# Second and third layer of the edge network: four 64x64 quadrant products against full-array products by a block-diagonal weight

## The chip, the cores and the metric

One core of a Trainium2 chip runs the whole program. Its engines are TensorE (PE in the views, with PEld for the loads of its stationary operand), VectorE (DVE), ScalarE (ACT), GpSimd (POOL) and the queues that start DMAs (SP and POOL). The metric is the device time of one execution in microseconds. The time before is the median of three runs.

## The reference, cut to what matters

Four stages follow one another on 1250 nodes of 512 features and 40000 edges: a segment mean, a mixture of experts, a graph network on the edges, and a second mixture of experts. The change lies in the third, in the small network that turns the 8 features of every edge into 512 weights:

```python
h = edge_feats                                   # [40000, 8]
for W in (W_mlp1, W_mlp2, W_mlp3):               # 8x64, 64x64, 64x64
    h = SILU_2MOM * jax.nn.silu(h @ W / jnp.sqrt(jnp.float32(W.shape[0])))
tpw = h @ W_mlp4 / jnp.sqrt(jnp.float32(W_mlp4.shape[0]))   # [40000, 512]
w1, w2, w3, w4 = jnp.split(tpw, 4, axis=-1)
s0 = x0[sender]; s1 = x1[sender]
# p1..p4: products of w1..w4 with the sender's features and the edge's 4 attributes
msg0 = jax.ops.segment_sum(m0, receiver, num_segments=num_nodes)
msg1 = jax.ops.segment_sum(m1, receiver, num_segments=num_nodes)
```

Everything is float32. The second and third layer multiply 64 hidden features by a 64x64 weight.

## The kernel before, in words

The edges are sorted by receiver into 352 tiles of 128 edges (`NTILE`). Four tiles make a step (`Q`, 88 steps, `STEPS`), eight a batch of the network (`BT`, 44 batches, `NB`). The loop over the steps is one pipeline of five engines.

**Network, layers 0 to 3 (`mlp_product`, L1686 on TensorE; `mlp_function`, L1326 on ScalarE).** Layer 0 turns the features of two batches round with one transpose (L1690). Layer 1 is four products with 64 rows of the array (L1696). The result of a batch is `act1`, 128 partitions by 512: partitions 0 to 63 hold the 64 hidden features of one half of the batch's 1024 edges, partitions 64 to 127 those of the other half. Layers 2 and 3 (both L1703) use four quadrants of 64x64 of the array: for each half `k` of the columns and each row half `h` a product of 64 rows, 64 columns of output and 256 moving columns, written to partitions 64k of bank 6 or 7 (the two banks of `pairs[3]`). So each of the two layers exchanges the places of edges between partitions and columns, and after both they are back. After each layer ScalarE applies silu from PSUM to `act1` (L1332), `act2` (L1334) or `act3` (L1336), one instruction of 128 by 512. A float32 product shows in the trace as two instructions on PE, each with its own load on PEld; the four quadrants of a layer show as 8 instructions.

**Last layer (`weights_of`, L1741).** For two tiles at a time it makes the 512 weights per edge in two banks: 64 rows, 128 columns of output, 512 moving columns, twice. A step has two such calls. Call `i` waits until VectorE is through with the messages of four tiles before (`v_msg`), as those four banks are a ring of two pairs.

**Messages (VectorE, `messages_of`, L1045 and L1048).** For two tiles at a time the weights in PSUM are multiplied by the gathered rows of the senders. It waits for `weights_of` (`p_tp`) and for the two gathers (`d_gat`). Once a step `picks_of` (L1032) and once in four steps `hot_of` (L1021) make parts of the stationary operand of the sum.

**Sum (TensorE, `sum_up`, L1758 and L1761).** For every step the messages are summed to 32 nodes by products with 32 columns of output, in four column tiles of the array. ScalarE then copies the sums out and scales what is carried on (L1403, L1406), and makes its share of the picks (L1391).

**Gathers (GpSimd, L1953).** One indirect DMA per tile into a ring of 8 tiles (`NGAT`); gather `i` waits until the messages of tile `i - 8` are made.

The order on TensorE in step `s` (L1765 and after) is: `weights_of` twice, then the products of the network that `mlp_order` (L146) gives to the gap of this step, then `sum_up(s - 1)`. With r = s // 2 + 1, an even step's gap holds layer 1 of batch r + 1 and layer 3 of batch r; an odd step's gap holds layer 2 of batch r + 1 and, in every second odd step, layer 0 of batches r + 2 and r + 3. Before the loop five places (L1724) hold the layers of batches 0 and 1 with which the loop begins, each after ScalarE's part of the place before. `spin` (L1473) issues products of 128x128 by 512 float32 columns whose results nobody reads: seven in step 0, three in step 88.

Of the kernel before, what the change touches and what calls it, by code (L numbers as in the profile page):

```python
# [13 lines left out]
ACT = mybir.ActivationFunctionType  # L14
# [37 lines left out]
MUL, HID = 128, 64  # L52
SILU_2MOM = 1.679177
# [4 lines left out]
ARENA = 42960  # L58
ZONE = HB * (4096 + 2048)
NW3 = 3  # L60
LATE = 2 * MUL + 2 * HID + 512 + 512
assert NB % 2 == 0 and NB * 64 + 2 * NTILE <= 4 * NPAD - LATE
NGAT, NSUM, NPICK, NHOT, HOT_STEPS = 8, 3, 3, 2, 4
PICKED = 2
# [93 lines left out]
def program(nc, consts, x, anc, sub, leaf_table, src, dst, ea4, ea8, gate, w13, w2, w_up, w_mlp1, w_mlp23,  # L158
            w_mlp4, w_out, ew, ei, v1, v2, out):
    ctx = ExitStack()  # L160
    with ctx:

        def sem(name):
            return ctx.enter_context(nc.semaphore(name))
# [7 lines left out]
        def carve(words, at=None):  # L172

            if at is None:
                at, top[0] = top[0], top[0] + words
                assert top[0] <= ARENA, top[0]
            return arena[:, at:at + words]

        def zone_of(at, size):

            used = [0]

            def take(words):
                used[0] += words
                assert used[0] <= size, (used[0], size)
                return carve(words, at + used[0] - words)

            return take

        def phase_tensors(**sizes):  # L190

            with ExitStack() as phase:
                return [phase.enter_context(nc.sbuf_tensor(n, [128, words], dt))[:, :]
                        for n, (words, dt) in sizes.items()]

        pairs = [ctx.enter_context(nc.psum_tensor(f"pair{i}", [128, 1024], F32)) for i in range(4)]
        banks = [pair[:, h * 512:(h + 1) * 512] for pair in pairs for h in range(2)]
# [103 lines left out]
        _, other_down1 = phase_tensors(other_gap1=(2048, F32), other_down1=(2048, F32))  # L301
        spare = zone_of(lnT_at, 4 * NPAD - LATE)
        other_spare, xS, hS = spare(2048), spare(512), [spare(512) for _ in range(2)]
# [3 lines left out]
        acc = dram("node_sums", [N + TILE, D])  # L307
        e_w = [carve(2048, zone + ZONE - 2048), carve(2048, edge_at)]
        late = zone_of(lnT_at + 4 * NPAD - LATE, LATE)
        wup_sb, m23_sb, m4_sb, wo_sb = late(2 * MUL), late(2 * HID), late(512), late(512)  # L310

        recs = carve(NREC * REC, edge_at).rearrange("p (s c) -> p s c", c=REC)
        table = dram("node_table", [N, 4 * MUL])
# [16 lines left out]
        act1, act2, fT, act3 = ring(512), ring(512), ring(128), [ring(512) for _ in range(2)]  # L330
# [4 lines left out]
        sum_pair, tp_pair, mlp_pair = pairs[0], pairs[1:3], pairs[3]  # L335
        tp_bank = banks[2:6]
        mlp_halves = mlp_pair[:, :].rearrange("p (h x) -> p h x", h=2)
        mlp_out = (banks[7][:, 256:384], mlp_halves[:, :, 0:256], mlp_halves[:, :, 0:256], mlp_halves[:, :, 256:512])
        oz = zone_of(zone, ZONE)
        sums_T = [oz(8 * MUL) for _ in range(2)]  # L340

# [57 lines left out]
        a_pick, a_mlp = sem("last_picks_made"), sem("mlp_activated")  # L399
# [759 lines left out]
        def scalar(a):  # L1159
# [63 lines left out]
            for k in range(NG):  # L1223
                if k >= 4:
                    a.wait_ge(p_start, k - 3)
                for c in range(4):
                    done = a.activation(out=diag[k % 4][:, c], in_=ident[:EP, :EP], func=ACT.Identity,
                                        scale=start_part[:, c % 2 * NW + 2 * k + c // 2:c % 2 * NW + 2 * k + c // 2 + 1])
# [97 lines left out]
            def mlp_function(r, layer):  # L1326
                b = mlp_out[layer]
                a.wait_ge(p_prod, mlp_done[r, layer])
                if layer == 0:
                    a.activation(out=fT, in_=b, func=ACT.Copy).then_inc(a_mlp, 1)  # L1330
                elif layer == 1:
                    a.activation(out=act1.rearrange("p (h x) -> p h x", h=2), in_=b, func=ACT.Silu, scale=8 ** -0.5).then_inc(a_mlp, 1)  # L1332
                elif layer == 2:
                    a.activation(out=act2.rearrange("p (h x) -> p h x", h=2), in_=b, func=ACT.Silu, scale=SILU_2MOM / 8).then_inc(a_mlp, 1)  # L1334
                else:
                    a.activation(out=act3[r % 2].rearrange("p (h x) -> p h x", h=2), in_=b, func=ACT.Silu,  # L1336
                                 scale=SILU_2MOM / 8).then_inc(a_mlp, 1)
# [42 lines left out]
            for place in mlp_first:  # L1380
                for r, layer in place:
                    mlp_function(r, layer)
# [27 lines left out]
            for s in range(STEPS + 1):  # L1410
                for r, layer in mlp_gaps[s] if s < STEPS else []:
                    mlp_function(r, layer)
                if s:
                    carry(s - 1)
                if s + 1 < STEPS:
                    picks_of(s + 1)
# [9 lines left out]
            def split_out(e):  # L1426
                if e:
# [6 lines left out]
                         scale=3 ** -0.5).then_inc(a_p4, 1)  # L1434
            for u in range(NT + 1):
# [5 lines left out]
                for h in range(2):  # L1441
                    done = a.activation(out=sums_T[u % 2][:, h * 512:(h + 1) * 512], in_=banks[2 * (u % 2) + h][:, :],
                                        func=ACT.Copy)
                done.then_inc(a_sums_T, 1)
                if u - 2 in TURNS_AT:
# [3 lines left out]
                                 in_=banks[6 + t % 2][:, :].rearrange("p (k n) -> p k n", k=4),  # L1449
                                 func=ACT.Copy).then_inc(a_xt, 1)  # L1450
# [18 lines left out]
        def tensor(pe):  # L1469
# [6 lines left out]
            for t in range(NT):  # L1476
                mm = pe.matmul(out=banks[2][:, t:t + 1], lhsT=in_sub[:, t * NP:(t + 1) * NP].bitcast(F32), rhs=K["sub512"],
                               start=True, stop=True)
# [9 lines left out]
            for t in range(NT):  # L1488
                if t >= 3:
                    pe.wait_ge(v_hit, t - 2)  # L1490
                if t == 7:
# [4 lines left out]
                          start=True, stop=True).then_inc(p_key, 1)  # L1496
# [14 lines left out]
            for t in range(NT):  # L1511
                g = slice(t % Q * WN, t % Q * WN + WN)
                pe.wait_ge(a_ln, t + 1)
                mm = pe.matmul(out=banks[0][g, :], lhsT=in_bound[:, t * WN:(t + 1) * WN], rhs=ln[:, t], start=t < Q,
                               stop=t + Q >= NT, skip_group_check=True)
            mm.then_inc(p_parts, 1)
            for t in range(NT):
                if t >= 3:
# [5 lines left out]
                          stop=True).then_inc(p_seg, 1)  # L1524
# [14 lines left out]
            for t in range(NT):  # L1539
# [3 lines left out]
                for k in range(4):  # L1543
                    mm = pe.matmul(out=banks[2][:, t * E0:(t + 1) * E0], lhsT=lnT[:, k, t * NP:(t + 1) * NP],
                                   rhs=gate_sb[:, k], start=k == 0, stop=k == 3)
# [3 lines left out]
                      skip_group_check=True)  # L1549
            pe.matmul(out=banks[6][:, E0:NT * E0], lhsT=ones, rhs=so_far_t[:, 0:NT - 1], start=False, stop=True,  # L1550
                      skip_group_check=True)
            pe.matmul(out=banks[7][:, 0:E0], lhsT=ones, rhs=so_far_t[:, NT - 1], start=True,
                      stop=True).then_inc(p_before, 1)
# [4 lines left out]
                      stop=True).then_inc(p_before, 1)  # L1558
            for k in range(NG):
                pe.wait_ge(a_diag, k + 1)  # L1560
                for c in range(4):
                    mm = pe.matmul(out=banks[3 + c // 2][:EP, 0:EJ], lhsT=diag[k % 4][:, c], rhs=marks[:, k],
                                   start=k + c % 2 == 0, stop=k == NG - 1 and c % 2 == 1)
# [123 lines left out]
            def mlp_product(r, layer):  # L1687
                b = mlp_out[layer]
                if layer == 0:
                    mm = pe.transpose(out=b, in_=feat[:, r * 64:(r + 2) * 64], identity=ident)  # L1690
                elif layer == 1:
                    for k in range(2):
                        q = r % 2 * 2 + k
                        for h in range(2):
                            p = slice(64 * h, 64 * (h + 1))
                            mm = pe.matmul(out=b[:, h, k * 128:(k + 1) * 128], lhsT=m1_sb[p, q * 128:(q + 1) * 128],  # L1696
                                           rhs=fT[p], start=True, stop=True, skip_group_check=True)
                else:
                    w, given = (m23_sb[:, 0:HID], act1) if layer == 2 else (m23_sb[:, HID:2 * HID], act2)
                    for k in range(2):  # L1700
                        for h in range(2):
                            p = slice(64 * h, 64 * (h + 1))
                            mm = pe.matmul(out=b[64 * k:64 * (k + 1), h], lhsT=w[p],  # L1703
                                           rhs=given[p, k * 256:(k + 1) * 256], start=True, stop=True,
                                           skip_group_check=True)
                return mm

            pe.wait_ge(a_y, FT)
# [3 lines left out]
            for t in range(NT):  # L1712
# [6 lines left out]
                for k in range(4):  # L1719
                    mm = pe.matmul(out=banks[2 + s][:, k * 128:(k + 1) * 128], lhsT=nT[s][:, k * 128:(k + 1) * 128],  # L1720
                                   rhs=wup_sb[:, 0:MUL] if k == 0 else wup_sb[:, MUL:2 * MUL], start=True, stop=True)
                mm.then_inc(p_up, 1)
            pe.wait_ge(g_packed, 4)
            for place in mlp_first:  # L1724
                if mlp_ahead[place[0]]:
                    pe.wait_ge(a_mlp, mlp_ahead[place[0]])
                for r, layer in place:
                    mm = mlp_product(r, layer)
                mm.then_inc(p_prod, 1)
# [39 lines left out]
            for s in range(STEPS + 1):  # L1769
                if s < STEPS:  # L1770
                    for i in range(s * Q, (s + 1) * Q, 2):
                        weights_of(i)
                    if mlp_gaps[s]:
                        pe.wait_ge(a_mlp, mlp_ahead[mlp_gaps[s][0]])
                        for r, layer in mlp_gaps[s]:
                            mm = mlp_product(r, layer)
# [50 lines left out]
            for t in range(NT):  # L1827
# [10 lines left out]
                for extra in extra_hl:  # L1838
                    mm = pe.matmul(out=bank[:, :], lhsT=extra_hot[t], rhs=extra, start=False, stop=True,
                                   skip_group_check=True)  # L1840
# [7 lines left out]
            for e in range(E1):  # L1848
                pe.wait_ge(v_w1, e + 1)
                for h in range(2):  # L1850
                    if e:
                        pe.wait_ge(a_gelu, 2 * (e - 1) + h + 1)
                    for k in range(4):
                        for a, b in PASSES:
                            mm = pe.matmul(out=banks[2 + h][:, :], lhsT=a1_hl[:, a, k, h * 128:(h + 1) * 128],  # L1855
                                           rhs=x_hl[:, b, k], start=k + a + b == 0, stop=k == 3 and a == 1)
                    mm.then_inc(p_h, 1)
                pe.wait_ge(v_w2, e + 1)
                for k in range(2):
                    pe.wait_ge(v_h, 2 * e + k + 1)  # L1860
                    for t in range(T5):
                        n = e * T5 + t
                        if e and k == 0:
                            pe.wait_ge(v_y, n - T5 + 1)
                        for a, b in PASSES:
                            mm = pe.matmul(out=banks[4 + n % 4][:, :], lhsT=h_hl[k][:, a, t * NP:(t + 1) * NP],  # L1866
                                           rhs=a2_hl[:, b, k], start=k + a + b == 0, stop=k == 1 and a == 1)
# [348 lines left out]
```

## Time and profile before

| | us |
|---|---|
| median of three runs (lowest, highest) | 1435.27 (1434.62, 1439.81) |
| the profiled execution, its own time | 1440.99 |
| its span, first to last instruction | 1439.1 |
| PE, PEld busy | 1353.6, 833.0 |
| DVE, ACT, POOL busy | 1151.2, 1003.0, 922.4 |

The page gives busy time per engine and the span in 40 slices. Matmuls are pipelined and their ends are modelled, so the busy time of PE contains the overlap with the next group; the distance from one group's start to the next group's start says what a group really takes. The loop over the steps runs from 833.2 us to 1305 us of the span.

### The profile page before, as it was taken

What the parts mean: (1) busy time and instruction counts of PE and PEld (TensorE: products, weight loads), DVE (VectorE), ACT (ScalarE), POOL (GpSimd) and SP (SyncE); (2) the same over time, 40 slices, a digit from 0 to 9 for tenths busy, and PEclk for the clock granted to TensorE, in tenths of its full rate; (3) what the DMA queues carried; (4) which work ended last, traced back from release to release, by engine and by line L of the source; (5) the groups of instructions that cost most, each with busy time, mean ns of one, the idle gap of its engine ahead of it and who ended that gap; (6) DMA issues with size and microseconds to landing.
All of it is one profiled execution on the core that took longest, in us unless ns stands there. A gap on an engine that the chain in (4) does not pass through costs nothing.

```text
span 1439.1 us, 24478 instructions
## 1 busy us (share of the span) xinstructions
PE 1353.6 (94%) x8774; PEld 833.0 (58%) x8774; DVE 1151.2 (80%) x1459; ACT 1003.0 (70%) x2000; POOL 922.4 (64%) x762
## 2 busy tenths in 40 slices
PE   4957999999899999999999699999999999998999
PEld 3454746888378874888567534434444443336887
DVE  7888927999089972999459769999999999995665
ACT  6237726888178863888457459999999999884433
POOL 4226675888888888888883467777777777762000
PEclk9859999999999999999999999999999999999999
DMA  9429476277827566765622769989999999985421
GB/s 331 155 92 334 134 243 239 37 272 278 294 34 282 187 232 187 281 215 158 182 62 49 238 189 306 306 296 307 309 305 303 307 307 293 294 291 176 144 89 59
DMA packets 91601, 316.54 MB, mean 220 GB/s; under 512 B 23754, under 2 KB 25988, under 8 KB 80859
## 3 DMA queue, kind: packets, MB, share of 16 engines
q1 hardware_dynamic: 45832, 202.57, 37.7%
q0 software_dynamic: 45648, 112.41, 28.7%
q8 instruction: 70, 1.15, 0.3%
q14 instruction: 51, 0.42, 0.1%
HBM read 378.96 MB, written 77.16 MB: 317 GB/s over the span
## 4 chain that ended last, share of the span: by engine, by line
PE 70%; DVE 11%; DMA 8%; POOL 5%; issue 4%; ACT 1%; SPq 0%; DVEq 0%; POOLq 0%; ACTq 0%
PE pair L1599 32%; PE pair L1741 7%; PE pair L1636 4%; PE pair L1761 4%; DMA arena<-node_table,arena 4%; POOL arena L1953 4%; DVE arena L1048 3%; PE pair L1758 3%; PE pair L1855 3%; PE pair L1866 3%; PE pair L1653 3%; PE pair L1703 2%; PE pair L1590 2%; POOL pair_rows L1906 1%; DVE arena L1045 1%
## 5 line engine op out<-in xcount | busy, mean ns | idle before, releaser
L1916 POOL DMA_INDIRECT sorted_edges<-arena x311 | 460.1, 1480 | 104.2 <-issue 96.0
L910 DVE TENSOR_TENSOR weights_hl<-arena,weights_hl 128x1024 fp32r<-128x1024 f32 x342 | 405.3, 1223 | 62.3 <-ACT weights_hl L1242 59.7
L1953 POOL DMA_INDIRECT arena<-node_table,arena x352 | 340.7, 968 | 129.6 <-issue 89.4
L1242 ACT ACTIVATE weights_hl<-arena 128x1024 fp32r<-128x1024 f32 x342 | 351.9, 1060 | 46.6 <-PE pair L1599 46.4
L1599 PE MATMUL pair<-weights_hl,rows_hl 128*128 128x512 f32 x1368 | 325.9, 395 | 4.3 <-ACT weights_hl L1242 3.0
L1048 DVE TENSOR_TENSOR arena<-pair,arena 128x1536 f32<-128x1536 f32 x176 | 307.7, 1748 | 0.0
L1599 PEld LDWEIGHTS pair<-weights_hl,rows_hl 128*128 128x128 f32 x1368 | 251.7, 188 | 69.8 <-DVE weights_hl L910 10.5
L1741 PE MATMUL pair<-arena 64*128 64x512 f32 x704 | 185.3, 634 | 7.2 <-DVE arena L1048 7.0
L1599 PE MATMUL pair<-weights_hl,hidden_hl 128*128 128x512 f32 x684 | 165.7, 395 | 0.0
L1391 ACT ACTIVATE arena<-arena 128x32 f32<-128x32 bf16 x704 | 157.8, 314 | 0.0
L1045 DVE TENSOR_TENSOR arena<-pair,arena 128x512 f32<-128x512 f32 x176 | 120.8, 686 | 29.5 <-PE pair L1741 19.8
L1599 PEld LDWEIGHTS pair<-weights_hl,hidden_hl 128*128 128x128 f32 x684 | 125.0, 188 | 25.6
L1761 PE MATMUL pair<-arena 128*32 128x256 f32 x2112 | 130.1, 379 | 0.0
L929 DVE TENSOR_TENSOR arena<-pair,arena 128x512 f32<-128x512 f32 x69 | 47.3, 686 | 101.8 <-ACT arena L1280 74.0
L1403 ACT ACTIVATE arena<-pair 128x512 f32<-128x512 f32 x176 | 105.1, 597 | 30.2 <-PE pair L1758 22.0
L1761 PEld LDWEIGHTS pair<-arena 128*32 128x32 f32 x2112 | 68.6, 110 | 82.9 <-issue 52.7
L1406 ACT ACTIVATE pair<-pair,arena 128x512 f32<-128x512 f32 x174 | 114.8, 660 | 0.0
L1741 PEld LDWEIGHTS pair<-arena 64*128 64x128 f32 x704 | 55.4, 186 | 99.8 <-DVE arena L1048 58.6
L1280 ACT ACTIVATE arena<-pair 128x512 f32<-128x512 f32 x69 | 41.3, 599 | 101.6 <-PE pair L1636 87.9
L1758 PE MATMUL pair<-arena 128*32 128x512 f32 x704 | 93.7, 604 | 0.0
L1636 PE MATMUL pair<-arena 128*64 128x512 f32 x352 | 88.9, 614 | 2.8 <-DMA arena<-in_w 2.8
L1926 POOL DMA_INDIRECT node_sums<-arena x27 | 52.2, 1932 | 51.4 <-ACT arena L1288 36.5
(292 smaller groups left out, 1541.0 us busy)
## 6 DMA issues: line engine op xcount, KB each, us to landing
arena<-in_w SPq DMA_DIRECT2D x73, 2048.0 KB, 8.6
arena<-in_w SPq DMA_DIRECT2D x85, 1024.0 KB, 9.2
sums<-arena SPq DMA_DIRECT2D x88, 512.0 KB, 5.7
other_down<-in_w SPq DMA_DIRECT2D x8, 1024.0 KB, 12.2
arena<-in_v SPq DMA_DIRECT2D x16, 512.0 KB, 4.6
pair_rows<-arena SPq DMA_DIRECT2D x1, 5934.0 KB, 26.2
arena<-pair_rows SPq DMA_DIRECT2D x23, 256.0 KB, 3.9
arena<-node_table,arena POOLq DMA_INDIRECT x352
```

What stands on the lines that cost most here:

```text
L910: v.tensor_tensor(out=part[s][:, 1], in0=by_chunk(n)[4], in1=part[s][:, 0].bitcast(F32), op=ALU.subtract).then_inc(v_low, 1)
L1045: v.tensor_tensor(out=m[:, :, 0:2], in0=w12, in1=rows_in[:, :, 0:1].to_broadcast([128, 2, 2, MUL]), op=ALU.mult)
L1048: v.tensor_tensor(out=m[:, :, 2:8].rearrange("p t (w m) u -> p t w (m u)", w=2), in0=w34.unsqueeze(2).to_broadcast([128, 4, 3, MUL]), in1= ...
L1242: a.activation(out=part[s][:, 0], in_=cols, func=ACT.Copy).then_inc(a_high, 1)
L1391: done = a.activation(out=picks[s % NPICK][:, j, c], in_=hot[s // HOT_STEPS % NHOT][:, s % HOT_STEPS, j], func=ACT.Copy, scale=recs[:, j * ...
L1599: mm = pe.matmul(out=bank[:, :], lhsT=st[:, a], rhs=part[s][:, w, half * 512:(half + 1) * 512], start=begins and (a, w) == (0, 0), stop=en ...
L1636: mm = pe.matmul(out=banks[2 + 2 * s + c][HALF * h:HALF * (h + 1), :], lhsT=xS[:, at:at + HALF], rhs=w[:, c], start=k == 0, stop=k == 3, s ...
L1741: mm = pe.matmul(out=tp_bank[(i + h) % Q], lhsT=act3[batch % 2][p, k * 128:(k + 1) * 128], rhs=m4_sb[p], start=True, stop=True)
L1758: mm = pe.matmul(out=bank, lhsT=pick, rhs=m[:, 1:5], start=s == 0, stop=True, skip_group_check=True)
L1761: mm = pe.matmul(out=bank.rearrange("p (b u) -> p b u", b=4)[:, c - 1:4:4 - c], lhsT=pick, rhs=m[:, 0:c + 5:c + 4], start=s == 0 and c == ...
L1916: g.indirect_dma_start(out=sorted_edges, out_offset=bass.IndirectOffsetOnAxis(ap=slot_i[:, j:j + 1], axis=0), in_=er[:, j, :], in_offset=N ...
L1953: g.indirect_dma_start(out=row, out_offset=None, in_=table, in_offset=bass.IndirectOffsetOnAxis(ap=senders[:, i:i + 1], axis=0)).then_inc( ...
```

## The change

The weights of layers 2 and 3 come from the host as two block-diagonal matrices of 128x128: W2 (or W3) at rows and columns 0 to 63 and again at 64 to 127. A batch's layer 2 becomes one product of 128 rows, 128 columns of output and 512 moving columns into bank 6, and layer 3 two products of 128x128 and 256 moving columns, into banks 6 and 7. Edges no longer change places between the two layers. The weight tile in SBUF grows from 128 to 256 columns; the tiles beside it move. ScalarE's silu of layer 2 reads one bank of 512 columns, where it read 256 columns of each of two.

```diff
-LATE = 2 * MUL + 2 * HID + 512 + 512
+LATE = 2 * MUL + 4 * HID + 512 + 512
@@
-        wup_sb, m23_sb, m4_sb, wo_sb = late(2 * MUL), late(2 * HID), late(512), late(512)
+        wup_sb, m23_sb, m4_sb, wo_sb = late(2 * MUL), late(4 * HID), late(512), late(512)
@@
-        mlp_out = (banks[7][:, 256:384], mlp_halves[:, :, 0:256], mlp_halves[:, :, 0:256], mlp_halves[:, :, 256:512])
+        mlp_out = (banks[7][:, 256:384], mlp_halves[:, :, 0:256], banks[6], mlp_halves[:, :, 256:512])
@@
-                    a.activation(out=act2.rearrange("p (h x) -> p h x", h=2), in_=b, func=ACT.Silu, scale=SILU_2MOM / 8).then_inc(a_mlp, 1)
+                    a.activation(out=act2, in_=b[:, :], func=ACT.Silu, scale=SILU_2MOM / 8).then_inc(a_mlp, 1)
@@
+                elif layer == 2:
+                    mm = pe.matmul(out=b[:, :], lhsT=m23_sb[:, 0:128], rhs=act1, start=True, stop=True)
                 else:
-                    w, given = (m23_sb[:, 0:HID], act1) if layer == 2 else (m23_sb[:, HID:2 * HID], act2)
-                    for k in range(2):
-                        for h in range(2):
-                            p = slice(64 * h, 64 * (h + 1))
-                            mm = pe.matmul(out=b[64 * k:64 * (k + 1), h], lhsT=w[p],
-                                           rhs=given[p, k * 256:(k + 1) * 256], start=True, stop=True,
-                                           skip_group_check=True)
+                    for h in range(2):
+                        mm = pe.matmul(out=b[:, h], lhsT=m23_sb[:, 128:256], rhs=act2[:, h * 256:(h + 1) * 256],
+                                       start=True, stop=True)
@@
-        w_mlp23=np.tile(np.concatenate([g["W_mlp2"], g["W_mlp3"]], 1), (2, 1)),
+        w_mlp23=np.concatenate([at_blocks((128, 128), g[f"W_mlp{n}"], [(0, 0), (HID, HID)]) for n in (2, 3)], 1),
```

## Rows read from the trace of the kernel before

**Rows 1.** Loop, busy time: stretch, length, PE, PEld, DVE, ACT, POOL, clock, DMA.
```profile
844.80:1285.70 440.90, 436.09 (x4387) 176.95 (x4388) 424.98 (x440) 403.11 (x1146) 323.45 (x334) 1.00 0.90 298
```

**Rows 2.** Chain of waits, one stretch of four steps: start us, us, what.
```profile
980.87 1.92 PE pair L1741 x8
982.78 0.59 PE pair L1703 x8
983.38 0.26 PE pair L1690
...
985.92 1.95 PE pair L1741 x8
...
988.32 0.59 PE pair L1703 x8
...
991.20 2.13 PE pair L1741 x8
...
996.22 1.99 PE pair L1741 x8
...
1001.54 0.62 PE pair L1741
```

**Rows 3.** Who waited for whom in the loop: total us, times, longest.
```profile
DVE arena L1045 <- PE pair L1741: 12.5, 19, 5.2
PE pair L1741 <- DVE arena L1048: 4.7, 7, 1.1
DVE arena L1045 <- DMA arena<-node_table,arena: 4.1, 6, 1.2
```

**Rows 4.** VectorE in order of time: start us, us, line, operation.
```profile
982.07 0.69 DVE L1045 TENSOR_TENSOR arena<-pair,arena 128x512 f32<-128x512 f32 x1 [0.42 <-PE pair L1741]
...
984.35 0.68 DVE L1045 TENSOR_TENSOR arena<-pair,arena 128x512 f32<-128x512 f32 x1
...
986.61 0.42 DVE L1032 TENSOR_TENSOR arena<-arena 128x256 f32<-128x256 bf16 x1
986.94 0.69 DVE L1021 TENSOR_TENSOR arena<-arena 128x512 bf16<-128x512 bf16 x1
987.54 0.68 DVE L1045 TENSOR_TENSOR arena<-pair,arena 128x512 f32<-128x512 f32 x1
```

**Rows 5.** TensorE in order of time: the spin of step 0, narrow windows.
```profile
838.63 6.28 PE L1473 MATMUL pair<-arena 128*128 128x512 f32 x14
...
843.89 1.02 PE L1473 MATMUL pair<-arena 128*128 128x512 f32 x2
...
844.32 0.59 PE L1473 MATMUL pair<-arena 128*128 128x512 f32 x1
844.84 1.99 PE L1741 MATMUL pair<-arena 64*128 64x512 f32 x8
```

**Rows 6.** TensorE: full-array products of 128 columns, then a transpose.
```profile
823.71 1.78 PE L1720 MATMUL pair<-arena 128*128 128x128 f32 x14
825.33 0.27 PE L1690 MATMUL pair<-arena 128*128 128x128 f32 x1
```

**Rows 7.** Instructions of TensorE in the loop by line.
```profile
L1703 PE MATMUL pair<-arena 64*64 64x256 f32 x672 | 55.7, 402 | 0.0
L1690 PE MATMUL pair<-arena 128*128 128x128 f32 x20 | 6.6, 328 | 0.0
```

**Rows 8.** VectorE, first message of step 1 and of step 85.
```profile
846.47 0.69 DVE L1045 TENSOR_TENSOR arena<-pair,arena 128x512 f32<-128x512 f32 x1 [5.18 <-PE pair L1741]
...
1285.74 0.69 DVE L1045 TENSOR_TENSOR arena<-pair,arena 128x512 f32<-128x512 f32 x1 [0.24 <-DMA arena<-node_table,arena]
```

**Rows 9.** TensorE before the loop and in step 0.
```profile
831.77 1.13 PE L1703 MATMUL pair<-arena 64*64 64x256 f32 x8 [1.21 <-ACT arena L1336]
832.83 0.47 PE L1690 MATMUL pair<-arena 128*128 128x128 f32 x1
...
837.80 0.90 PE L1703 MATMUL pair<-arena 64*64 64x256 f32 x8
```

## The prediction, made before the changed kernel ran

> **What bounds the kernel now.** I read the busy times of the loop first: it takes 440.9 us of the span from 844.8 to 1285.7, and PE is busy 436.1 of it, VectorE 425.0, ScalarE 403.1, GpSimd 323.5 [rows 1]. The reader is to see that two engines are within 4% of full, so that busy time alone can't say which of them sets the pace. GpSimd's figure leaves out the time between its gathers.
>
> Then the chain of waits over four steps in the middle [rows 2]. In steady running it stays on TensorE. The starts of the four blocks of `weights_of` (L1741) at 980.87, 985.92, 991.20, 996.22 and 1001.54 give steps of 5.05, 5.28, 5.02 and 5.32 us, together 20.67. I use these four steps as the unit, because they hold two batches of the network: two layers 2, two layers 3, two layers 1, one layer 0.
>
> How much of the 20.67 does TensorE wait? The block after 980.87 lasts 1.92 and the same block after 991.20, with the same kind of group behind it, 2.13: 0.21 of waiting there. The two blocks in front of layer 1 last 1.95 and 1.99. One such block is four streams of 0.43 and one load of 0.11 (below), 1.83; 0.10 more belongs to it in this view, since the chain begins the next group of the same shape 0.1 later than it starts; so 0.02 and 0.06 are waits. Sum 0.3 us; TensorE without any wait would need 20.67 - 0.3 = 20.37.
>
> VectorE's own need [rows 4]: a pair of messages takes 984.35 - 982.07 = 2.28 and 986.61 - 984.35 = 2.26, the picks 986.94 - 986.61 = 0.33, and once in four steps the one-hot 987.54 - 986.94 = 0.60. Four steps need 4 x (2.27 + 2.27 + 0.33) + 0.60 = 20.08. That is 0.3 us less than TensorE's need, and the first row shows which one is late: the first message of the step waited 0.42 us for `weights_of`. Over the whole loop the waits say the same [rows 3]: the messages waited 12.5 us for `weights_of` and 4.1 us for gathers, `weights_of` 4.7 us for messages. TensorE sets the pace, with little to spare behind it.
>
> The unit doesn't hold everywhere. From the first message of step 1 at 846.47 to that of step 85 at 1285.74 are 439.3 us [rows 8] for 84 steps or 21 units; 21 x 20.67 = 434.1. The other 5.2 us are stretches in which a gather lands late and VectorE then is late for TensorE.
>
> **Price of the new products.** A layer is now 8 instructions on four quadrants, 0.59 us from its start to the next group's; so both for the layer 2 at 982.78 and the layer 3 at 988.32 [rows 2], and 672 instructions or 84 groups of it lie in the loop [rows 7]. What the new form costs is told best by the spin, which has its shape: 128 rows, 128 columns of output, 512 float32 columns, two instructions each [rows 5]. From the start at 843.89 to that at 844.32 are 0.43 us per instruction. From the first start 838.63 to the last 844.32 are 5.69, which is 13 x 0.43 and 0.1: before the first stream a load of the weights is exposed, 0.11. From the last start to the next group of another shape are 844.84 - 844.32 = 0.52, 0.09 more than the stream. So a full-array product alone between groups of other shapes costs 0.11 + 2 x 0.43 + 0.09 = 1.06 us.
>
> Layer 2 in a step without layer 0: 0.59 becomes 1.06, +0.47. Layer 2 in front of layer 0: today 0.59 + 0.26 = 0.85 [rows 2]. The transpose has the shape of the new product. Where it follows such products today, 14 products of 128 columns and the transpose start evenly (825.33 - 823.71 = 1.62, 0.115 each), with no load to be seen in front of it [rows 6]; so its 0.26 falls to 0.15 and the layer's 0.09 goes: 0.97 + 0.15 = 1.12, +0.27. Layer 3: two products of 256 columns, four instructions of half the stream, 0.11 + 4 x 0.215 + 0.09 = 1.06, +0.47. No row shows a full-array product of 256 columns. From below, with no exposed load and no gap at either end, it is 0.86, +0.27; from above, if each of the two products paid its load and its gap, 0.86 + 0.4 = 1.26, +0.67. I take +0.47, as the stream goes with the columns between the rows of 128 (0.115) and 512 (0.43).
>
> The Trainium skill (TensorEngine Tiling (Array Packing), Key Properties) has that a change of tiling mode, not only of tile, drains TensorE. The 0.09 and 0.11 around the spin agree. By that rule the change takes one of the two switches around every second layer 2 away, which is the 0.2 by which that case is cheaper, and alters nothing else in number.
>
> **What the loop makes of it.** A unit of TensorE's work becomes 20.37 + 0.27 + 0.47 + 2 x 0.47 = 22.05 us. VectorE's stays 20.08, so it has 2 us per unit to spare and TensorE's 0.3 of waiting goes: the step with the one-hot needs 5.47 on VectorE, and TensorE's own step there is 5.05 + 0.27 = 5.32, 0.15 shorter, but the next one is 5.75, and two steps of PSUM lie between the two. So 22.05 against 20.67, +1.38 for a unit and +29.0 for 21. Late gathers: what waits for a gather is VectorE, mostly by about 1 us or less (longest 1.2 of 6 waits [rows 3]), and 2 us of slack in a unit take nearly all of that; of the 5.2 us I leave 0.5, -4.7. GpSimd has more time per gather, ScalarE too; its silu waits for the end of the gap's products and then runs while `sum_up` does, as now. Loop: +24.3.
>
> Before the loop the layers are on the path, each waiting for ScalarE [rows 9]. Layers 2 and 3 of batch 0 come at full speed, +0.47 each until the result. Layer 2 of batch 1 at 831.77 runs at the clock's lower level (1.2 GHz in place of 2.4): to the transpose at 832.83 are 1.06 us for the 8 instructions that take 0.59 in the loop. The new one needs 0.11 + 2 x 0.86 = 1.83, less 0.11 of load in front of the transpose, +0.65. Sum 1.6. In step 0 the layer 3 at 837.80 took 0.83 (to the spin at 838.63), partly at half clock; new 1.06 at full and 2.0 at half, +0.2 to +1.2, of which 0.4 disappear because the message at 846.47 [rows 8] came 0.4 after the product before it was done (844.84 + 0.11 + 2 x 0.43 + 0.16, what an instruction lasts beyond its stream, [rows 5]). I take +1.4 for all before step 1, with 0.8 and 2.6 as ends.
>
> After step 85 no products of the network remain, and the last three steps wait for gathers: nothing. The larger weight tile adds 64 KB to one transfer that is issued long before the loop: nothing, 0.2 us if it were waited for. ScalarE's silu from one bank in place of two: 512 columns as before, nothing.
>
> Sum: +24.3 + 1.4 = +25.7 us. The profiled execution took 1440.99 (span 1439.1), so its like is 1466.7 (span 1464.8). The median of the three runs is 5.7 lower: 1435.3 + 25.7 = **1461.0**.
>
> **Rivals.**
> *Hidden, not slower.* VectorE or the ring of gathers sets the pace, and TensorE's longer gap falls into its waiting. For it: VectorE busy 96%, DMA 0.90, late gathers. Against it: TensorE's waits are 0.3 us in 20.67 and it would have to take 1.65. It decides where TensorE's need for a unit stays under the 20.67 of now; the price then is 0 to 1.4, 1435 to 1437. The Trainium skill (Perfetto Trace Analysis, Identifying the Most-Contended Engine) calls matmul busy time a bad measure of TensorE's load and wants that of the weight loads in its place. Here the loads are busy 177.0 of 440.9 us, 40% [rows 1], by which VectorE would be the bound and this rival true. The distances of starts speak against that. Chance 4%.
>
> *Cheaper switches.* The load and the gap around the new products hide as they do between groups of one shape: 0.86 for each, +0.27 in place of +0.47 for 22 layers 2 alone and 42 layers 3, -12.8, and 0.2 less before the loop: +13, 1448. For it: the load of the next weights is hidden inside the spin. Against: the spin's own first load is not. Chance 9%.
>
> *Nothing given back.* Late gathers and waits for messages stay what they are: 22 x 0.47 + 20 x 0.27 + 42 x 0.47 = +35.5 in the loop and up to 2.6 before it, 1473. It would hold if the ring of gathers were tied to TensorE's order by more than messages. Chance 8%. Products of 256 columns at the upper price of 1.26 give 42 x 0.2 = 8.4 more, 1469; 4%.
>
> **How the numbers follow.** The forecast has 75%, its own range 1455 to 1467. The range that should hold 8 in 10 leaves out most of the first, half of the second and the worst of the last rivals: 1450 to 1469. A difference of 0.5%, 7.2 us, is what can be told from no change here (the three runs span 5.2 us). Slower by more than that: all but the hidden case, 0.95; within it 0.04; faster 0.01, since no part takes anything from any engine but 0.1 us of load before every second layer 0.
>
> **What would show it.** Right: line by line, the layer 2 group as 2 instructions and 1.06 us to the next start, layer 3 as 4 and 1.06, the transpose 0.15; a unit of four steps of 22.0 to 22.1 us; VectorE waiting for `weights_of` in every step, some 35 us over the loop in place of 12.5, and for gathers under 2; `weights_of` waiting for messages under 2. Wrong: a unit that stays near 20.7, VectorE without longer waits, or groups of 0.86.

## The result, and the profile after

| | before | after |
|---|---|---|
| median, us (lowest, highest; 4 runs each) | 1435.78 (1434.62, 1439.81) | 1460.22 (1459.27, 1463.27) |
| the profiled execution, its own time, us | 1440.99 | 1459.27 |
| its span, us | 1439.1 | 1457.3 |

The ratio is 1.0175, 95% interval 1.0156 to 1.0194: slower by 24.4 us. The forecast was 1461.0 and slower.

Chain of waits of the changed kernel, four steps, where [rows 2] has those of before. Line 1739 is `weights_of`, 1699 layer 2, 1702 layer 3, 1690 layer 0:

```profile
981.85 1.92 PE pair L1739 x8
983.76 1.05 PE pair L1699 x2
984.82 0.11 PE pair L1690
...
987.22 1.92 PE pair L1739 x8
...
989.58 1.06 PE pair L1702 x4
...
992.93 1.92 PE pair L1739 x8
994.85 1.06 PE pair L1699 x2
...
998.20 1.92 PE pair L1739 x8
...
1003.91 1.92 PE pair L1739 x8
```

Read two things here. The groups of two and four instructions last 1.05 and 1.06 us where the eight quadrant instructions lasted 0.59. And all blocks of `weights_of` last 1.92 us, where before they had 1.92, 1.95, 2.13 and 1.99: TensorE waits for nobody. From 981.85 to 1003.91 are 22.06 us, against 20.67.

The waits in the loop of the changed kernel, total us, times, longest (to compare with [rows 3]), and its busy times ([rows 1]):

```profile
POOL arena L1951 <- DVE arena L1048: 60.9, 85, 1.2
...
DVE arena L1045 <- PE pair L1739: 36.0, 62, 1.0
...
DVE arena L1045 <- DMA arena<-node_table,arena: 1.9, 3, 0.9
...
PE pair L1739 <- DVE arena L1048: 0.6, 1, 0.6
```
```profile
844.80:1303.30 458.50, 457.92 (x3920) 203.18 (x3920) 421.23 (x436) 405.48 (x1141) 321.87 (x333) 1.00 0.89 286
```

These waits are taken up to 1308 us, a little behind the loop; up to 1303.3 us, as far as [rows 3] goes in the kernel before, they are 35.6 (61 times), 1.3 (2 times) and 0.6. So VectorE's wait for `weights_of` went from 12.5 to 35.6 us, that for gathers from 4.1 to 1.3, TensorE's for messages from 4.7 to 0.6. The weight loads are busy 203 of 458 us, 44%, in a stretch in which TensorE has no gap left.

The loop's ends in VectorE's order of time, as in [rows 8]:

```profile
839.87 0.69 DVE L1045 TENSOR_TENSOR arena<-pair,arena 128x512 f32<-128x512 f32 x1 [4.83 <-PE pair L1739]
...
1303.33 0.69 DVE L1045 TENSOR_TENSOR arena<-pair,arena 128x512 f32<-128x512 f32 x1 [0.32 <-PE pair L1739]
```

463.5 us in place of 439.3: the loop took 24.2 more. 21 x 22.06 = 463.3, so the 5.2 us that the loop took beyond its undisturbed units, put down to late gathers, fell to 0.2.

The whole of the two profiled executions: up to the start of layer 0 of batches 0 and 1 (825.33 before, 817.71 after) the changed kernel is 7.6 us earlier, in stages that the change doesn't touch; from there to the first message of step 1 it takes 22.2 us in place of 21.1, +1.0; in the loop +24.2; behind it +0.6. Since layer 0 that is +25.8. The 7.6 us go the other way, and these two executions differ by only 18.3 us; the medians differ by 24.4. Runs of the kernel before spread over 5 us by themselves.

### The profile page after: what moved, and what is told of

The parts are those of the page before. It is cut to its first block, busy times and chain, and to the rows that moved or that the text cites. A ratio compares the mean times of both kernels' runs of the same rounds, so it can differ in the third digit from the quotient of the medians.

```text
span 1457.3 us, 23598 instructions
## 1 busy us (share of the span) xinstructions
PE 1379.8 (95%) x8334; PEld 862.1 (59%) x8334; DVE 1152.0 (79%) x1459; ACT 1008.6 (69%) x2000; POOL 918.4 (63%) x762
## 4 chain that ended last, share of the span: by engine, by line
PE 84%; DVE 6%; DMA 4%; POOL 2%; issue 2%; ACT 1%; SPq 0%; DVEq 0%; POOLq 0%; ACTq 0%
PE pair L1599 32%; PE pair L1739 11%; PE pair L1759 7%; PE pair L1756 6%; PE pair L1636 5%; PE pair L1702 3%; PE pair L1699 3%; PE pair L1853 3%; PE pair L1864 3%; PE pair L1653 3%; PE pair L1590 2%; POOL pair_rows L1904 1%; PE pair L1696 1%; PE pair L1805 1%; DMA arena<-node_table,arena 1%
## 5 line engine op out<-in xcount | busy, mean ns | idle before, releaser
L1739 PE MATMUL pair<-arena 64*128 64x512 f32 x704 | 176.5, 618 | 3.5 <-DVE arena L1048 3.5
L1739 PEld LDWEIGHTS pair<-arena 64*128 64x128 f32 x704 | 60.4, 186 | 83.9 <-issue 55.7
L1636 PE MATMUL pair<-arena 128*64 128x512 f32 x352 | 85.8, 599 | 0.3 <-DMA arena<-in_w 0.3
```

What stands on the lines that cost most here:

```text
L1636: mm = pe.matmul(out=banks[2 + 2 * s + c][HALF * h:HALF * (h + 1), :], lhsT=xS[:, at:at + HALF], rhs=w[:, c], start=k == 0, stop=k == 3, s ...
L1739: mm = pe.matmul(out=tp_bank[(i + h) % Q], lhsT=act3[batch % 2][p, k * 128:(k + 1) * 128], rhs=m4_sb[p], start=True, stop=True)
```

## The experiments

They ran on several chips, and the kernel before shows two times: on three chips, called slow below, it takes 1604.8, 1616.4 and 1615.8 us, on the others 1436 to 1437. Each kernel is compared with the kernel before on its own chip. "Unit" is the time of four steps in the middle of the loop in which nothing is late.

**1. Layer 2 alone, slow chip.** The edit, on the changed kernel:

```diff
-                    for h in range(2):
-                        mm = pe.matmul(out=b[:, h], lhsT=m23_sb[:, 128:256], rhs=act2[:, h * 256:(h + 1) * 256],
+                    for k in range(2):
+                        for h in range(2):
+                            p = slice(64 * h, 64 * (h + 1))
+                            mm = pe.matmul(out=b[64 * k:64 * (k + 1), h], lhsT=m23_sb[p, 128 + 64 * h:192 + 64 * h],
+                                           rhs=act2[p, k * 256:(k + 1) * 256], start=True, stop=True,
```

> Only layer 2 has the new form; layer 3 keeps the four quadrants, so that edges come out in each other's places and the output differs. Theory (TensorE sets the pace, its idle is given back before the time grows): four steps need 20.37 + 0.27 + 0.47 = 21.11 us on TensorE against 20.67 now, +9.2 over 21 units, of which late gathers give back 3 to 4; +1.1 before the loop. Sum +6 to +8 us, 1442 to 1444. Rival (nothing is given back, each product adds its price): 22 x 0.47 + 20 x 0.27 + 1.1 = +17, 1453. Rival (VectorE or the gathers set the pace up to some point): 0 to +2.

Measured: 1601.84 us against 1604.76, ratio 0.9989 (0.9976 to 1.0001).

**2. Layer 3 alone, slow chip.** Layer 2 goes back to quadrants, with the same kind of edit, and its silu and banks with it.

> Only layer 3 has the new form; layer 2 keeps the four quadrants, and the output differs for the same reason. Theory: 20.37 + 2 x 0.47 = 21.31 us for four steps, +13.4 over 21 units, less 4 for late gathers, +0.7 before step 1: +9 to +11 us, 1445 to 1447. Rival (nothing given back): 42 x 0.47 + 0.7 = +20.4. If the theory holds, this and the run with layer 2 alone sum to about +17, less than the +24.4 of both together, because each has the same 0.3 us per unit and the same late gathers to give back.

Measured: 1603.55, ratio 0.999 (0.9977 to 1.0003).

**3. Full array, half of the columns, slow chip.**

```diff
-                    mm = pe.matmul(out=b[:, :], lhsT=m23_sb[:, 0:128], rhs=act1, start=True, stop=True)
+                    mm = pe.matmul(out=b[:, 0:256], lhsT=m23_sb[:, 0:128], rhs=act1[:, 0:256], start=True, stop=True)
@@
-                    for h in range(2):
-                        mm = pe.matmul(out=b[:, h], lhsT=m23_sb[:, 128:256], rhs=act2[:, h * 256:(h + 1) * 256],
+                    mm = pe.matmul(out=b[:, 0], lhsT=m23_sb[:, 128:256], rhs=act2[:, 0:256], start=True, stop=True)
```

> The changed kernel with full-array products over half of the columns only: layer 2 one product of 256 columns, layer 3 one product of 256 (the other half of the hidden features is left out). Theory (the price is the streamed columns, 0.43 us per 256 float32 columns, whatever share of the array they use): a layer costs 0.11 + 0.43 + 0.09 = 0.63 us against 0.59 for four quadrants; unit 20.37 + 0.04 - 0.16 + 0.08 = 20.33, time as before the change within 3 us, 1433 to 1439. Rival (the full-array shape, the block-diagonal load or silu reading one bank costs by itself): stays above 1445.

Measured: 1601.78, ratio 0.9974 (0.9963 to 0.9986).

**4. Quadrants of 32 columns, slow chip.** On the kernel before:

```diff
-                            mm = pe.matmul(out=b[64 * k:64 * (k + 1), h], lhsT=w[p],
-                                           rhs=given[p, k * 256:(k + 1) * 256], start=True, stop=True,
+                            mm = pe.matmul(out=b[64 * k:64 * (k + 1), h, 0:32], lhsT=w[p],
+                                           rhs=given[p, k * 256:k * 256 + 32], start=True, stop=True,
```

> The kernel before with each quadrant product over 32 of its 256 columns (the rest of layers 2 and 3 is left out). TensorE's need for four steps falls by about 4 x 0.38 to 18.9 us. Theory: VectorE's 20.08 sets the pace then, 21 x (20.67 - 20.08) = 12 us less, of which more late gathers take some back: -6 to -12 us, 1424 to 1430. Rival (gathers hold 20.67 anyway): 1433 to 1437.

Measured: 1603.2, ratio 0.999 (0.9975 to 1.0004). Neither more nor less work on TensorE moves the time on this chip by more than 3 us (experiment 3, with more work than the kernel before, is 3.0 us faster, and the cause of that is not known). So the four say nothing on the theories; they show that another thing holds the loop there. What it is stays open (last section).

**5. float32r products.** On the changed kernel; `phase_tensors` makes tensors of their own type, and ScalarE rounds the weights once:

```diff
-        act1, act2, fT, act3 = ring(512), ring(512), ring(128), [ring(512) for _ in range(2)]
+        _, _, fT, act3 = ring(512), ring(512), ring(128), [ring(512) for _ in range(2)]
+        _, act1, act2, m23r = phase_tensors(below_acts=(2048, F32), act1_r=(512, F32R), act2_r=(512, F32R),
+                                            w23_r=(4 * HID, F32R))
@@
+            a.wait_ge(d_late, 64)
+            a.activation(out=m23r, in_=m23_sb, func=ACT.Copy)
             for place in mlp_first:
```

and `m23r` for `m23_sb` in the products of layers 2 and 3.

> The changed kernel with the operands of layers 2 and 3 written as float32r (silu writes act1 and act2 so, the weights are rounded once by ScalarE before the loop), in tensors of their own; a product is then one instruction of 0.216 us for 512 columns, as for the experts' products in this trace, and not two of 0.43. Theory where TensorE sets the pace (before: 1435.8): layer 2 alone 0.11 + 0.22 + 0.09 = 0.42 us against 0.59 on quadrants, in front of layer 0 0.33 + 0.15 = 0.48 against 0.85, layer 3 0.42 against 0.59; TensorE needs 20.37 - 0.17 - 0.37 - 0.34 = 19.5 for four steps, under VectorE's 20.08, which then sets the pace: -6 to -12 us, 1424 to 1430. Rival (gathers hold the loop): no change, within 3 us of the kernel before. On the chip where the kernel before takes 1604.8 us and no edit of these layers moved it, every theory expects no change.

Measured: 1432.22 against 1437.06 us, ratio 0.9968 (0.995 to 0.9986), 4.8 us faster than the kernel before. TensorE in order of time, one layer 2 (L1703) and one layer 3 (L1706) with the next start behind each:

```profile
985.90 0.50 PE L1703 MATMUL pair<-act_r,w_r 128*128 128x512 f32 x1
986.34 1.06 PE L1760 MATMUL pair<-arena 128*32 128x512 f32 x8
...
991.21 0.50 PE L1706 MATMUL pair<-act_r,w_r 128*128 128x256 f32 x2
991.64 1.06 PE L1760 MATMUL pair<-arena 128*32 128x512 f32 x8
```

A layer takes 0.43 to 0.44 us; 0.42 was worked out. But the unit is 20.49 us, not near VectorE's 20.08, and the gain is less than forecast. GpSimd starts a gather every 1.26 us in this kernel with hardly a break. One gather of the 16 in a unit takes 1.20 us in place of 0.95, and sixteen starts, from 1003.29 to 1023.78 us, take 20.49 us, as long as the unit. VectorE waits for one of them in the unit:

```profile
1014.93 0.41 DVE L1034 TENSOR_TENSOR arena<-arena 128x256 f32<-128x256 bf16 x1
1015.70 0.69 DVE L1047 TENSOR_TENSOR arena<-pair,arena 128x512 f32<-128x512 f32 x1 [0.36 <-DMA arena<-node_table,arena]
```

So the rival's engine was there after all, 0.2 us per unit under the 20.67 of the kernel before, and the theory's step that VectorE would be next was wrong: GpSimd comes first, with VectorE 0.4 us under it.

**6. Layer 2 alone**, the kernel of experiment 1 on another chip.

> Only layer 2 in the new form, the same kernel as in the first study of it, which fell on a chip where the kernel before takes 1604.8 us. Where the kernel before takes about 1436: theory (TensorE sets the pace, its idle is given back before the time grows) four steps of 21.11 us, 21 x 0.44 = +9.2, 3 to 4 of it given back by late gathers, +1.1 before the loop: +6 to +8 us. Rival (each product adds its price, nothing given back): +17. Rival (VectorE or gathers set the pace up to some point): 0 to +2.

Measured: 1447.34 against 1436.1 us, ratio 1.0075 (1.0053 to 1.0098), +11.2; expected were +6 to +8. The undisturbed unit is 21.13, as expected. Between the first message of step 1 and that of step 85 lie 449.0 us; 21 x 21.13 = 443.7, and 5.3 us are left beyond the units, as many as before the change (5.2): VectorE waited 7.6 us for gathers,

```profile
DVE arena L1045 <- PE pair L1742: 14.2, 44, 0.5
DVE arena L1045 <- DMA arena<-node_table,arena: 7.6, 15, 1.1
...
PE pair L1742 <- DVE arena L1048: 1.0, 2, 0.6
```

The miss is there: with 1.0 us of slack for VectorE in a unit (21.13 - 20.08) nothing was given back. How much slack it takes is not shown. What is left beyond the units in one profiled execution each is 5.2 us at 0.6 of slack (before), 2.6 at 0.7 (experiment 8), 5.3 at 1.0 (here), 2.5 at 1.5 (experiment 7) and 0.2 at 2.0 (the whole change).

**7. Layer 3 alone**, the kernel of experiment 2 on another chip.

> Only layer 3 in the new form, the same kernel as before on the slow chip. Where the kernel before takes about 1436: theory four steps of 21.31 us, +13.4, less 4, +0.7: +9 to +11 us. Rival (nothing given back): +20. By the theory this one and layer 2 alone sum to about +17, less than the +24.4 of both together.

Measured: 1451.61, ratio 1.0104 (1.0076 to 1.0131), +15.5; expected were 9 to 11. The unit is 21.61 in place of 21.31. TensorE, steps in which both engines wait:

```profile
985.05 2.02 PE L1744 MATMUL pair<-arena 64*128 64x512 f32 x8
986.90 0.61 PE L1696 MATMUL pair<-arena 64*128 64x128 f32 x8
...
995.59 2.28 PE L1744 MATMUL pair<-arena 64*128 64x512 f32 x8
997.71 0.61 PE L1696 MATMUL pair<-arena 64*128 64x128 f32 x8
```

The same block of `weights_of` takes 986.90 - 985.05 = 1.85 us to the next group once and 997.71 - 995.59 = 2.12 the other time: TensorE waits 0.3 us there for messages, while VectorE has waited 1.0 and 0.4 us for `weights_of` in the same unit:

```profile
981.26 0.69 DVE L1045 TENSOR_TENSOR arena<-pair,arena 128x512 f32<-128x512 f32 x1 [0.99 <-PE pair L1744]
...
992.07 0.69 DVE L1045 TENSOR_TENSOR arena<-pair,arena 128x512 f32<-128x512 f32 x1 [0.39 <-PE pair L1744]
```

Layer 3 lies in the even steps alone, which TensorE now makes in 5.7 us, and the odd ones stay at 4.8 and 5.05, under VectorE's 4.87 and 5.47. Each engine is late in turn, and the unit is longer than the longer of the two sums. Adding layer 2's 0.74 us of work to this kernel, which gives the changed kernel, lengthens the unit by 22.06 - 21.61 = 0.45 only: it fills those waits. The two halves of the change cost 11.2 and 15.5 us, together 26.7. The expectation had about 17, less than the 24.4 of the whole; it is more, because nothing came back of the late gathers in experiment 6, half of it here, and 0.3 us of waits stay in every unit here.

**8. Full array, half of the columns**, the kernel of experiment 3 on another chip.

> The changed kernel with full-array products over half of the columns (half of the hidden features of layers 2 and 3 left out), the same kernel as before on the slow chip. Theory (the price is the streamed columns): 0.63 us a layer, four steps of about 20.5 with VectorE's and GpSimd's needs so near, within 3 us of the kernel before. Rival (the full-array shape, the block-diagonal load or silu reading one bank costs by itself): over 8 us above the kernel before.

Measured: 1438.24, ratio 1.0016 (1.0 to 1.0032), +2.1. TensorE, one layer 3 and one layer 2 and the next starts:

```profile
983.45 0.70 PE L1701 MATMUL pair<-arena 128*128 128x256 f32 x2
984.08 1.06 PE L1754 MATMUL pair<-arena 128*32 128x512 f32 x8
...
988.44 0.70 PE L1699 MATMUL pair<-arena 128*128 128x256 f32 x2
989.07 1.06 PE L1754 MATMUL pair<-arena 128*32 128x512 f32 x8
```

0.63 us each, as worked out, and the unit 20.74. So the full-array shape, the load of 128 columns, and silu's read from one bank together cost 2.1 us, at most 4.6 by the interval: the price of the change is that the array streams 512 columns where it streamed 256 in all four quadrants at once.

**9. Layer 3 beside layer 2**, on the kernel before. In every second batch the transpose of layer 0 overwrites a part of layer 3's result, which changes the output and not the amount of work.

```diff
-        gap = [(r + 1, 1), (r, 3)] if s % 2 == 0 else [(r + 1, 2)] + ([(r + 2, 0)] if r % 2 == 0 else [])
+        if s % 2 == 0:
+            gap = [(r + 1, 1)] if r + 1 < NB else [(r, 3)]
+        else:
+            gap = ([(r, 3), (r + 1, 2)] if r + 1 < NB else []) + ([(r + 2, 0)] if r % 2 == 0 else [])
```

> The kernel before with layer 3 moved into the odd step's gap in front of layer 2, so that both groups of quadrants stand side by side: one change of shape less per batch (0.09 of gap and 0.05 of load). TensorE needs 20.37 - 0.28 = 20.09 us for four steps. The run with float32r products took 20.49 for four steps although TensorE needed less, so 20.49 is what the other engines allow. Theory: 21 x (20.67 - 20.49) = 4 us less, late gathers as before: -2 to -5 us. Rival: the three silus after one gap (two of 0.6 us, one of 0.27) come in front of ScalarE's carrying of the sums and delay sum_up: slower, +3 to +10 us.

Measured: 1439.22, ratio 1.0021 (1.0004 to 1.0039), 3.1 us slower where 2 to 5 faster were expected. TensorE:

```profile
981.98 1.13 PE L1744 MATMUL pair<-arena 64*128 64x512 f32 x4 [0.17 <-DVE arena L1051]
983.04 1.09 PE L1706 MATMUL pair<-arena 64*64 64x256 f32 x16
984.07 1.07 PE L1761 MATMUL pair<-arena 128*32 128x512 f32 x8
```

The two layers side by side take 984.07 - 983.04 = 1.03 us, 0.15 less than 2 x 0.59, as worked out. The unit nevertheless is 20.91, 0.24 longer than before. TensorE waits for messages in front of the second half of `weights_of` in the odd steps, behind even steps that it makes in 4.65 us, under VectorE's 4.87. Over the loop these waits are 9.2 us in 41 of them, against 4.7 in 7 before. The rival named ScalarE for the same sign, and in the loop TensorE never waits for it. It is what experiment 7 has, steps of very unequal work on TensorE.

**10. Quadrants of 32 columns**, again.

> The kernel before with each quadrant product of layers 2 and 3 over 32 of its 256 columns (the rest of those layers is left out), the same kernel as before on the slow chip. Where the kernel before takes about 1436: TensorE needs about 18.9 us for four steps. The float32r run stood at 20.49 with TensorE at 19.5. Theory (another engine's need, not TensorE's, is met at 20.49, and that is all that layers 2 and 3 can give): 20.45 to 20.50 here too, -3 to -7 us. Rival (20.49 was still TensorE's coupling to VectorE): the unit falls on towards VectorE's 20.08, -9 to -13 us.

Measured on a slow chip: 1618.31 against 1616.38, ratio 1.0018 (0.9997 to 1.0039). It tells nothing of the theories.

**11. Layer 2 twice.** On the changed kernel:

```diff
-                    mm = pe.matmul(out=b[:, :], lhsT=m23_sb[:, 0:128], rhs=act1, start=True, stop=True)
+                    for _ in range(2):
+                        mm = pe.matmul(out=b[:, :], lhsT=m23_sb[:, 0:128], rhs=act1, start=True, stop=True)
```

> The changed kernel with layer 2's full-array product issued twice into the same bank: two more instructions of 0.43 us per batch, same shape, no new gap. TensorE needs 22.06 + 2 x 0.86 = 23.78 us for four steps. Theory (with the change TensorE alone sets the pace and hides nothing more): unit 23.7 to 23.8, 21 x 1.72 = +36 on the changed kernel and +1.5 before the loop, +60 to +63 on the kernel before: 1496 to 1499. Rival (some of it still falls into waits, as each half of the change showed 0.2 to 0.3 us of waits in its unit): below +55.

Measured on the same slow chip as experiment 10: 1615.15, ratio 0.9989 (0.9964 to 1.0014).

**12. Layer 2 twice**, again.

> The changed kernel with layer 2's full-array product issued twice, the same kernel as before on the slow chip, where it cost nothing. Where the kernel before takes about 1436: TensorE needs 22.06 + 2 x 0.86 = 23.78 us for four steps. Theory (with the change TensorE alone sets the pace and hides nothing more): unit 23.7 to 23.8, 21 x 1.72 = +36 on the changed kernel and +1.5 before the loop, +60 to +63 on the kernel before: 1496 to 1499. Rival (some of it still falls into waits, as layer 3 alone in the new form left 0.3 us of waits in its unit): below +55.

Measured on a third slow chip: 1614.39 against 1615.84, ratio 0.9996 (0.9981 to 1.001). The layer's four instructions there take the 1.83 us that 0.11 + 4 x 0.43 gives, up to the transpose:

```profile
1010.00 1.98 PE L1700 MATMUL pair<-arena 128*128 128x512 f32 x4
1011.83 0.27 PE L1690 MATMUL pair<-arena 128*128 128x128 f32 x1
```

That is 1.24 us more than the 0.59 of four quadrants, where the change alone adds 0.47, and layer 3 has its new form too. Nothing of it reaches the time on such a chip. What the doubled layer costs where TensorE sets the pace was not measured.

## Why the prediction was right

**The price of the products: right.** A layer 2 without layer 0 behind it costs 0.47 more: 1.06 where 0.59 was. Layer 3 the same, 1.06; its 256-column form, which no row showed, went by the columns. In front of layer 0 the pair of groups takes 1.05 + 0.11 = 1.16 us in the chain's view, 1.12 were forecast. Experiment 8 shows the cause by taking half of the columns away: 0.63 us and a kernel like that of before.

**The unit: right, 22.06 against 22.05.** The sum rested on TensorE losing all of its 0.3 us of waits. It did (0.6 us left in the whole loop). That this was no matter of course is seen in experiment 7, where the same rule failed by 0.3. It failed where the even steps became longer and TensorE made the odd ones in less than VectorE needs. It came out in experiment 6, where layer 2 lengthens only the odd steps, which had been the shorter ones: all four then take 5.24 to 5.38 us. In the whole change every step of TensorE but one is longer than VectorE's 4.87 or 5.47 (5.37, 5.71, 5.27 and 5.71 us), and VectorE has 2 us to spare in the unit.

**Late gathers given back: right in sum, on thin ground.** Of 5.2 us 0.2 are left; 0.5 were forecast. Experiment 6, with 1.0 us of slack per unit, gave nothing back, and over the experiments what is left does not fall evenly with the slack. The prediction gave no measure of how much slack a late gather needs, so that nearly all of it came back is in part luck.

**The loop: +24.3 forecast, +24.2 measured.**

**Before the loop: +1.4 forecast, +1.0 measured, by deviations that offset each other; the agreement is luck.** From layer 0 to `weights_of` of step 0 the profiled executions took 7.9 us before and 10.5 after, +2.6 and not +1.6, because layer 3 of batch 0 ran at the clock's lower level as well (granted 0.50 of full from 822.72 us on), 2.07 us:

```profile
822.72 2.07 PE L1702 MATMUL pair<-arena 128*128 128x256 f32 x4
825.96 2.07 PE L1699 MATMUL pair<-arena 128*128 128x512 f32 x2 [1.17 <-ACT arena L1336]
...
831.17 1.13 PE L1702 MATMUL pair<-arena 128*128 128x256 f32 x4
```

In return the clock was back at 2.4 GHz for half of the first `weights_of`, for layer 1 and for the layer 3 of step 0 (1.13 us at 831.17). From `weights_of` of step 0 to the first message of step 1 it was 11.7 us in place of 13.2, 1.5 less. Three steps of the forecast for this stretch don't hold. It let 0.4 us disappear between the last product before step 1 and its message: from the start of `weights_of` of step 1 to that message are 1.63 us in both executions, so nothing disappeared. Its terms add up to 1.4 to 2.4, of which it took the lowest without a reason. And it let the clock fall where it had fallen before. That place changes from run to run: in the profiled executions of experiments 6 and 7 the granted clock is 1.00 all the way, and the stretch from layer 0 to the first message of step 1 takes 18.8 us in each, less than the 21.1 of the kernel before.

**The rivals.** Hidden: false where the kernel takes 1436 us, and true on the chips where it takes 1605 to 1616. There experiments 1 and 2 show either half of the change for nothing, and experiments 11 and 12 the whole change with its layer 2 doubled on top; the change by itself was not run there. Cheaper switches: false, load and gap were paid each time. Nothing given back: false for the whole change; for layer 2 alone in experiment 6 it is true of the late gathers and false of the waits (unit 21.13, not 20.67 + 0.74 = 21.41). The Trainium skill (Perfetto Trace Analysis, Identifying the Most-Contended Engine) judges TensorE's headroom by the share of peak arithmetic and the busy share of weight loads. The prediction applied the second alone, and the loads' 40% spoke for hidden. The trace doesn't agree: at 44% TensorE was without a gap. The share of peak arithmetic was not worked out here.

**A faster kernel.** Experiment 5 beats both: 0.9968 (0.995 to 0.9986) of the time of before. It owes that to one instruction per product in place of two, so that a layer takes 0.43 to 0.44 us. Whether the quadrants could have float32r too was not measured.

## What to carry to other kernels

Price a product by the columns that the array streams and by what stands around it, from the distances of starts in the trace: four quadrants at once with 256 columns each took 0.59 us, a full-array product of 256 columns 0.63, one of 512 columns 1.06. A block-diagonal weight pays for half an array of zeros. When two engines are within a few per cent, sum each one's own need over the smallest period that repeats and take the larger. Then compare them step by step as well: where one engine's short steps fall under the other's need and its long ones lie above, as in experiments 7 and 9, the period is longer than either sum. And look at which chip ran: a price that is exact on one can be hidden whole on another.

## What the runs showed that was not expected

On three chips all kernels took 1600 to 1618 us. The stages before the loop are nearly as long as elsewhere (the first `weights_of` at 831.7 to 840.4 us). The loop is what is longer, 598 to 612 us between step 1 and step 85 against 434 to 463. Once in nearly every pair of steps, some 14 us apart, VectorE stands still for 3 to 7 us, mostly about 4.5, and ScalarE and GpSimd stand still beside it; TensorE works on for a part of that time and then has gaps of up to about 1 us. For more than half of these waits the profile can't say what VectorE waited for, and calls it remote; most others it puts down to `weights_of`. VectorE and GpSimd of experiment 12:

```profile
1004.27 0.69 DVE L1045 TENSOR_TENSOR arena<-pair,arena 128x512 f32<-128x512 f32 x1 [4.52 <-remote]
```
```profile
1000.13 0.95 POOL L1952 DMA_INDIRECT arena<-node_table,arena  x1 [0.30 <-issue]
1001.39 0.95 POOL L1952 DMA_INDIRECT arena<-node_table,arena  x1 [0.30 <-issue]
1006.90 0.95 POOL L1952 DMA_INDIRECT arena<-node_table,arena  x1 [4.55 <-DVE arena L1048]
```

GpSimd waits there for the messages before it reuses a place of its ring, and it stops later than VectorE (at 1002.3 us, VectorE at 999.8). Whether the gathers issued before land late there the profile doesn't show. So the cause is open; no experiment was made on it.
